# A hybrid transformer layer on one core: the first two row pairs of each attention batch turned by VectorE and a way through device memory

## What is computed

```
x = x + attn_a(layernorm(x))
x = x + ffn(layernorm(x))
x = x + attn_b(layernorm(x), W_q, W_k, W_v, W_o)
x = x + ffn(layernorm(x))

attn_b: Q = x W_q;  K = x W_k;  V = x W_v
        attn = softmax(Q K^T / sqrt(512));  out = (attn V) W_o
ffn:    down(silu(gate(x)) * up(x)),  width 1408
```

## Time and profile before

| | |
|---|---|
| median of 3 runs | 932.37 us (932.2 to 932.9) |
| profiled execution | 933.69 us |
| its span | 931.9 us |
| TensorE busy | 918.5 us, 99% |
| VectorE / ScalarE / GpSimd busy | 630.9 / 444.3 / 429.5 us |
| transfers | 61.75 MB, 29.2% of 16 engines' span on SP's queue |

### The profile page before, as it was taken

One profiled execution on the slowest core, in us unless ns is written; L12 is line 12 of the kernel. 1 busy time (PEld: TensorE's weight loads), 2 busy tenths in 40 slices (PEclk: granted clock), 3 DMA queues, 4 the chain that ended last, 5 costly groups with the idle time before them and its releaser, 6 DMA issues.

```text
span 931.9 us, 13051 instructions
## 1 busy us (share of the span) xinstructions
PE 918.5 (99%) x4534; PEld 513.7 (55%) x4550; DVE 630.9 (68%) x1171; ACT 444.3 (48%) x884; POOL 429.5 (46%) x448
## 2 busy tenths in 40 slices
PE   7999999999999999999999999999999999999998
PEld 4888888888743444444444444444444444444444
DVE  6555666848777687777754878547776777765643
ACT  4433334356567723664343445324444685346620
POOL 5442424466547645665640143420515566546530
PEclk9999999999999999999999999999999999999999
DMA  9401300024031172003812728215471002910001
GB/s 318 181 13 34 135 15 34 1 80 148 13 124 46 24 120 39 2 0 57 125 46 46 113 46 153 52 23 95 65 113 24 1 1 34 192 46 1 1 34 57
DMA packets 239952, 61.75 MB, mean 66 GB/s; under 512 B 226768, under 2 KB 227088, under 8 KB 239504
## 3 DMA queue, kind: packets, MB, share of 16 engines
q1 hardware_dynamic: 239888, 60.92, 29.2%
HBM read 41.47 MB, written 19.43 MB: 65 GB/s over the span
## 4 chain that ended last, share of the span: by engine, by line
PE 87%; DVE 5%; POOL 2%; SPq 2%; issue 2%; ACT 1%; DMA 1%; DVEq 0%; POOLq 0%
PE psum L2327 49%; PE psum L2574 14%; PE psum L2576 13%; PE psum L2724 8%; PE psum L2376 1%; PE psum L2365 1%; SPq L801 1%; SPq L820 1%; PE psum L2461 1%; DVE ln_bn L1620 1%; DVE wv_lo L1711 1%; DMA xres<-x 1%; DVE s_f L2155 0%; DMA turned<-blocks 0%; POOL hid L1034 0%
## 5 line engine op out<-in xcount | busy, mean ns | idle before, releaser
L1038 POOL TENSOR_TENSOR hid<-hid,hid_hi 128x512 f32<-128x512 f32 x88 | 102.9, 1169 | 104.1 <-DVE hid_hi L1976 104.1
L2574 PE MATMUL psum<-xf,w_gu 128*128 128x512 f16 x352 | 133.9, 380 | 0.7 <-DVE yt L2058 0.7
L2574 PE MATMUL psum<-xf,w_s 128*128 128x512 f16 x264 | 100.1, 379 | 1.5 <-DVE up L1949 1.3
L2576 PE MATMUL psum<-xf,w_gu 128*128 128x512 f16 x264 | 100.1, 379 | 0.0
L2327 PE MATMUL psum<-wd_low,hid_lo 128*128 128x512 bf16 (+1 forms) x330 | 73.8, 373 | 0.2
L1361 ACT ACTIVATE hid_lo<-hid 128x512 f16<-128x512 f32 x88 | 54.9, 624 | 33.1 <-POOL hid L1038 33.1
L1034 POOL TENSOR_TENSOR hid<-up,gate 128x512 f32<-128x512 f32 x44 | 56.0, 1272 | 25.2 <-ACT gate L1356 25.2
L2576 PE MATMUL psum<-xq,w_s 128*128 128x512 f16 x176 | 66.7, 379 | 0.0
L2574 PEld LDWEIGHTS psum<-xf,w_gu 128*128 128x128 f16 x352 | 34.3, 97 | 55.4 <-ACT acc L1346 15.5
L1356 ACT ACTIVATE gate<-gate,sg_xs 128x512 f32<-128x512 f32 x44 | 31.7, 721 | 58.6 <-DVE gate L1959 58.6
L2327 PEld LDWEIGHTS psum<-wd_low,hid_lo 128*128 128x128 f16 x330 | 32.2, 98 | 36.9
(11 more groups left out here) (354 smaller groups left out, 2414.9 us busy)
## 6 DMA issues: line engine op xcount, KB each, us to landing
prob_blocks<-probs SPq DMA_DIRECT2D x60, 128.0 KB, 2.8
back<-prob_blocks SPq DMA_DIRECT2D x40, 128.0 KB, 3.0
turned<-blocks SPq DMA_DIRECT2D x36, 128.0 KB, 3.2
cla_wide<-cla_dram SPq DMA_DIRECT2D x16, 256.0 KB, 3.3
out<-xres SPq DMA_DIRECT2D x15, 256.0 KB, 2.0
xres<-x SPq DMA_DIRECT2D x3, 1024.0 KB, 13.0
blocks<-xn SPq DMA_DIRECT2D x24, 128.0 KB, 3.0
codes_gu<-gateT SPq DMA_DIRECT2D x1, 2816.0 KB, 11.6
```

The source lines that it names most:

```text
L1038: nc.gpsimd.tensor_tensor(hid[:, :], hid[:, :], hid_part(hid_hi, j, half), ALU.subtract).then_inc(rest_done, 1)
L2574: nc.tensor.matmul(bank(use[0]), w, x_operand(piece, k, False), start=start and k == 0, stop=False, skip_group_check=not start)
L2576: last = nc.tensor.matmul(bank(use[0]), w, x_operand(piece, k, True), start=False, stop=k == 1, skip_group_check=not start)
```

## The change

Pairs 0 and 1 of B1 and of F2 (SENT = 2) leave TensorE. VectorE turns their 32x32 blocks in xn (`pair_turned`), SP sends them out (`pair_to_dram`) and back (`pair_to_slot`) into x_first, which is now 1024 columns wide, and ScalarE and VectorE read both halves from there instead of from PSUM. Since one xn serves all pairs, the next normalisation waits until the pair before has left (pair_out). Pairs 2 and 3 stay on TensorE.

```diff
+            def pair_to_dram(q, i):
+                sp.wait_ge(pair_blocks_done, sent_n(q, i) + 1)
+                src = xn[:, :].rearrange("p (m j) -> p m j", j=SQ)
+                for a in range(QUADS):
+                    sp.dma_start(pair_blocks[sent_n(q, i), a].rearrange("m (c i) j -> i (m c) j", c=QUADS),
+                                 src[a * SQ:(a + 1) * SQ, :, :]).then_inc(pair_out, 16)
+            def pair_to_slot(q, i):
+                sp.wait_ge(pair_out, sent_all(q, i))
+                if i > 0:
+                    sp.wait_ge(x_ab_lo, n)
+                    sp.wait_ge(x_t34_done, 2 * n)
+                    sp.wait_ge(pair_2_lo, sent_n(q, i))
...
+            def pair_turned(q, i):
+                dve.wait_ge(ln_xn_done, ln_n("X", q, 2 * i + 1) + 1)
+                nc.vector.transpose(xn[:, :], xn[:, :]).then_inc(pair_blocks_done, 1)
+
             def x_normalise(q, i):
+                if q in (B1, F2) and 0 < i <= SENT:
+                    dve.wait_ge(pair_out, sent_all(q, i - 1))
...
-                x_both(0)
+                x_row_highs(q, 0)
...
-                turn_both(0)
...
-                turn_both(1)
```

More of the change, by code:

```diff
@@ L514, in x_2_cols, with sent, sent_n, sent_all @@
         return slice(0, 4 * P) if q in (B0, B1) else slice(2 * P, 4 * P)
+    def sent(q, i):
+        return q in (B1, F2) and i < SENT
+    def sent_n(q, i):
+        return (q == F2) * SENT + i
+    def sent_all(q, i):
+        return TURN_DMAS * (sent_n(q, i) + 1)
+    def pair_slot(q):
+        return x_first[X_PLACE[q]]
     def x_first_of(q, i):
[L517 removed]
+        return slot[i][:, 0:D] if q in MOVED else x_first[X_PLACE[q]][:, 0:D]
     def x_pair(t, first, i):
@@ L877, in _ @@
                     weights_back(0)
[L878 to L882, removed]
+                    for b, s in enumerate((B1, F2)):
+                        probs_to_dram(b, 0)
+                        probs_back(b, 0)
+                        probs_to_dram(b, 1)
+                        probs_back(b, 1)
+                        if b == 1:
+                            down_scales()
+                        probs_to_dram(b, 2)
+                        pair_to_dram(s, 0)
+                        probs_back(b, 2)
+                        probs_to_dram(b, 3)
+                        pair_to_dram(s, 1)
+                        pair_to_slot(s, 0)
+                        probs_back(b, 3)
+                        probs_to_dram(b, 4)
+                        pair_to_slot(s, 1)
+                        probs_back(b, 4)
+                        probs_to_dram(b, 5)
+                        probs_back(b, 5)
+                        probs_to_dram(b, 6)
+                        probs_back(b, 6)
+                        if b == 0:
+                            weights_back(1)
+                            probs_to_dram(b, 7)
+                            probs_back(b, 7)
             store(0, *range(BT))
@@ L1113, in pairs_of @@
                     x_12_low(q, i)
+                    if i == 0:
+                        x_rstd(q, *range(4, 8))
             def weight_sums(*which):
@@ L1155, in x_copy @@
                     act.wait_ge(x_t34_done, 2 * n)
-                nc.scalar.activation(x_first[X_PLACE[q]][:, :], bank(first[0]), ACT.Copy).then_inc(drained[first[0]], 1)
+                nc.scalar.activation(x_first_of(q, i), bank(first[0]), ACT.Copy).then_inc(drained[first[0]], 1)
             def x_row_highs(q, i):
@@ L1656, in x_second @@
                     done = x_2_lo_done
+                elif sent(q, i):
+                    dve.wait_ge(pair_back, sent_all(q, i))
+                    t, first, done = pair_slot(q)[:, D:2 * D], x_first_of(q, i), pair_2_lo
                 else:
@@ L1659, in x_second @@
                     Use(dve, phase, b).read_out(one)
-                    t, first, done = bank(two[0]), x_first[v][:, :], drained[two[0]]
+                    t, first, done = bank(two[0]), x_first_of(q, i), drained[two[0]]
                 dve.wait_ge(x_b2_hi, n + 1)
@@ L2265, in _ @@
                 row_max(3)
-                x_normalise(q, 0)
                 p_blocks(3)
-                for l in range(4, 8):
-                    x_stats(q, l)
+                x_normalise(q, 1)
+                pair_turned(q, 1)
                 query_parts(b, 1, 0)
```

63 lines of the change are left out of this document (45 added, 18 removed).

## The result

The changed kernel takes 935.88 us (median of 6 runs, 935.21 to 939.28); the kernel before took 932.63 beside it. By the medians it is 3.25 us slower, where 931.0 was forecast, and outside the range of 929.3 to 934.0. The ratio on record is formed from the single executions and not from the medians; it is 1.0041, with a 95% interval of 1.0025 to 1.0056. One execution of the kernel before (1188 us, beside experiments 9 to 12) and the profiled one of experiment 12 (3400 us) were disturbed; both are left out of every figure, and the trace of experiment 12 is not read.

A forecast was written before the change was run, and what follows sets the result against it. TensorE's queue was taken to bound the kernel, provided its helpers keep up. Of 4.32 us removable, 0.15 (batch 0) plus 1.2 (batch 1) = 1.35 us would remain, off a median of 932.37: 931.0 us, range 929.3 to 934.0.

The forecast's parts named there:

- What bounds the kernel, and what can be gained: TensorE's queue bounds the time; removing 16 turns a batch can gain 2.16 us a batch, 4.32 in all, no more.
- First place: Turns ahead of the scores, 1.29 us a batch; s_lo is late next, so 0.6 in batch 0, 1.0 in batch 1.
- by 0.5: VectorE's second normalisation finds xn free: pair 0 has left by 530.6, VectorE comes at 531.1, on time by 0.5.
- Second place: Turns before the scores of rows 6 and 7; of 0.87 us only 0.2 comes in, bounds 0 and 0.87.
- The tail: Up to the sixth context tile: of batch 0's 0.8 gain only 0.15 is left; batch 1 keeps 1.2.
- 7.19 us without gap: VectorE from its split of row 5 (574.2) to that of row 6 (581.4), batch 0: 7.19 us, as before.
- 571.9: Batch 0's tail: query row 5 comes back about 571.9, and ScalarE then splits it.
- 562.0: Batch 0's tail: the leg out of query row 5 starts at 561.22 + 0.8 = 562.0.
- the 0.15: Batch 0's remaining gain: sixth context tile ready at 582.8, against a start at 582.95 before.
- so its 1.2 stays: Batch 1's tail: row 6's split has 1.45 of room before the sixth tile, so the 1.2 us gain stays.
- The rival "slower" (0.13): SP's single queue makes every leg take 5.94; batch 0 loses 2.3, batch 1 1.5; 936.2 us, chance 0.13.
- 572.1: Point in batch 0 from which row 5 coming back later costs one microsecond of time per microsecond.

The follow-up runs named there:

- Kernel 9: Kernel 8 with the second product of query rows 6 and 7 computed before the first; 931.05 us (-1.72), in a later session 932.49 (-0.55).
- experiment 10: Kernel before, with three unused row maxima on VectorE ahead of query row 7's in each batch, so TensorE waits; 939.75 us (+6.98).
- experiment 11: Kernel before, with the same three row maxima as experiment 10 and 24 unused identity turns on TensorE inside each wait; 939.05 us (+6.28).
- experiment 12: Changed kernel with one pair sent (SENT = 1), pair 1 back on TensorE, both VectorE's and ScalarE's orders of before; 931.62 us (-1.15).
- experiment 5: Changed kernel with 16 unused identity turns ahead of the scores of query rows 4/5 and of 6/7 in each batch; 937.71 us (+4.53).
- experiment 13: Kernel 8 with the products of query rows 6 and 7 in the order 2, 1, 3, 6, 5; 931.84 us (-1.20).
- kernel 8: Changed kernel with VectorE's and ScalarE's orders of before, and pair 1's way back ahead of row 4's leg out; 932.80 us (-0.38), later 932.25 (-0.79).
- experiment 1: Changed kernel with VectorE normalising pair 3 ahead of query row 4's output addition, as before; 935.60 us (+2.67).
- experiment 3: Changed kernel with both orders of before at the tail, VectorE's and ScalarE's; 934.83 us (+1.90).
- experiment 2: Changed kernel with ScalarE's order of before: pair 1's last parts and the partial sum ahead of query row 5's split; 934.98 us (+2.05).
- experiment 7: Changed kernel with pair 1's way back issued ahead of query row 4's leg out on SP's queue; 934.84 us (+1.66).
- experiment 6: Kernel before with only the change's two tail orders on VectorE and ScalarE, no pair sent; 934.57 us (+1.39).
- experiment 4: Changed kernel with 16 unused identity turns inside each of TensorE's waits, at batch 0's sixth context tile and batch 1's last softmax; 937.92 us (+4.99).

## Why the prediction was wrong

**What bounds the kernel, and what can be gained: right in the main.** TensorE's queue sets the time where its helpers keep up: 64 unused turns added to the changed kernel's cost 1.3 us (experiment 5), and the shorter first place is seen in every profile with the change.

**First place: right in its numbers, with one wrong link.** I gave it 0.6 and 1.0; it brought 0.59 and 1.28. (The scores behind it are those of query rows 4 and 5, not 2 and 3.) In batch 1 the query parts start 0.63 earlier against TensorE's second context tile, as I had it (0.65), and nothing waits. In batch 0 they start 0.11 earlier, not 0.25, and the third product waits 0.46 for s_lo. The second normalisation was to find xn free "by 0.5"; it waited for pair 0's leg:

```profile
530.90 1.00 DVE L1712 TENSOR_SCALAR xn<-xres,xmv,xrstd 128x512 f32<-128x512 f32 x2 [0.83 <-DMA pair_blocks<-xn]
```

That 0.6 came out all the same is in part luck.

**Second place: a wrong place, by a small amount.** I looked at the third product and gave the place 0.2 a batch. The product that can't start earlier is the first: it reuses the bank of the product just before, and ScalarE's emptying lies between them. TensorE now waits there:

```profile
554.83 0.38 PE L2813 MATMUL psum<-xb_hi,a_hi 128*128 128x512 f16 x1 [0.78 <-ACT probs L1564]
```

From the product before it to the next context tile it took 8.72 us before and takes 8.71 now. The eight turns of 0.87 had stood in a wait and their removal was worth nothing; experiment 13, which takes that wait away on top of kernel 8, shortens the same stretch to 7.77. Zero was within my bounds (0 to 0.87).

**The tail: this is the step that failed.** I let VectorE reach row 5 at 574.2 and added "7.19 us without gap" to 581.4. It reached row 5 at 575.07 and row 6 at 583.37. Of the 1.97, the leg is one part: the split of row 5 on ScalarE was 0.96 later than my 571.9, since SP issued row 5's way out 0.4 later than my 562.0, behind row 4's slow way back, and the two legs took longer. The other is the 7.19 itself, which became 8.30. I had counted the operations that the change orders anew at the durations that they had in the old order; the normalisation's 1.44 was that of its place beside GpSimd's short operations, and it costs 2.57 one output addition later. Experiments 1, 3 and 8 (1.44) against 2 and 7 (2.57 and 2.56 in batch 0), and experiment 6 (2.57 without a pair sent), show that in batch 0 the order makes the difference, with or without the legs. ScalarE's order I had priced (2.3 from its split to VectorE's; 2.21 measured), but as something batch 0 could pay. Its room was also smaller than I took it: I read the sixth tile's start as 582.95 from the chain of waits, and the timeline has 582.78. With that, not even the 0.15 is left.

**Batch 1: "so its 1.2 stays" was wrong.** I looked at one waiter, the sixth tile. The delay on VectorE also delays the row maximum of row 7, then the softmax, and batch 1 has a turn of row 7's probabilities ahead of the sixth tile: it waited 2.03 for a consumer that stood in no sum.

**The rival "slower" (0.13)** had SP's queue right as one of two causes: row 5 was back at 572.86, past its 572.1, and the earlier way back of pair 1 takes off 1.6. It had every leg at 5.94, which did not happen, and not VectorE's part. Its price of 936.2 is close to the 935.88 measured, by a sum of other terms. What I missed is that there are two causes: with one order put right +2.05 or +2.67 of the +3.25 stays, with the leg alone +1.66, with all three nothing (-0.38).

**The clock** was in none of my cases. In the executions where it fell it costs up to 3.55 us, which explains the upper end (939.28 and 937.35, mean clock 0.996 and 0.998), not the median.

## What to carry over

An operation on VectorE has its duration at its place: before moving one that reads and writes only SBUF, look at what GpSimd does in the stretch it moves to. A wait that the trace does not show may stand behind work that fills it; before that work is removed, trace for the next instruction, and not only for a later one, what released it. With one queue for all transfers, put a transfer that is free to go ahead of the ones that the critical chain needs later, and price a delay at every consumer behind it.

## What was not expected of the hardware

- **VectorE beside GpSimd.** Two normalising operations of 128x512 took 0.96 to 1.00 us alone, 1.44 beside GpSimd's operations of 0.72 and 0.91, and 2.57 and 2.83 beside its longer ones. A subtraction of 0.42 took 1.87 beside one of 2.54, in the kernel before too. In every one of the cases beside GpSimd VectorE ended 0.28 to 0.29 us after an operation of GpSimd had ended (577.72 after 577.44 in the kernel before, 580.26 after 579.98 in the changed one, 665.45 after 665.16 in experiment 4), and GpSimd's operations next to them grew as well (0.73 to 0.91, 1.16 to 1.35). The Trainium skill (SBUF — State Buffer, Who interferes with whom) says that the two share a pair of SBUF ports as an exclusive lock, for VectorE's fast modes and for two SBUF inputs, and that issue order decides who blocks. The numbers here agree: VectorE's operation does not slow down by a share, it ends when GpSimd's has ended.
- **TensorE's clock.** Behind the wait of 2.06 us in the changed kernel the granted clock fell to half (1.2 GHz of 2.4) about 1 us after work had begun again (us, TensorE busy, clock, DMA share, GB/s):

```profile
583.00:584.00 1.00, 0.38 (x2) 1.00 0.00 0
584.00:585.00 1.00, 1.00 (x6) 0.81 0.00 0
585.00:586.00 1.00, 1.00 (x3) 0.50 0.01 3
...
588.00:589.00 1.00, 1.00 (x6) 0.98 0.84 129
```

  In this profile the wait of 2.03 in batch 1 did the same; the wait of 2.6 in experiment 10 did not and that of 2.8 did. The Trainium skill (TensorE: Matmul & The Clock Gate, Part 1: The HAM clock gate) has the same two levels and ties them to how busy the engine has been; experiments 10 and 11 agree.
- **One kernel, two sessions.** Kernel 9 was 1.72 under the kernel before in one session and 0.55 in another on another chip, with the same code and 11 runs each. Differences of about a microsecond between sessions say little here, whatever their intervals.
